# Spreading the closing averages and moments of a graph attention kernel over the last 47 steps of its softmax loop

## The chip, the cores and the metric

The kernel runs on one core of a Trainium2 chip. The metric is the device time of one execution in microseconds (us); shorter is better. PE is the matrix engine, DVE the vector engine, ACT the scalar engine, POOL is GpSimd and SP the engine that here only issues DMAs. PEld is the loading of weights into PE.

## What is computed

Two rounds of message passing over a graph with 6250 nodes and 100,000 edges, each followed by a layer normalisation over 128 features:

```python
edge_index = jnp.stack([src, dst])
x = _layernorm(x + _L0_gnn_ref(x, edge_attr_128, L0_gnn_fc_w, L0_gnn_attn, edge_type_100, src, dst), axis=-1)
x = _layernorm(x + _L1_gnn_ref(x, edge_index, L1_gnn_W, ...), axis=-1)
# the second round, in _L1_gnn_ref:
h = features @ W.T + b
s1 = h @ a1_w + a1_b[0]
s2 = h @ a2_w + a2_b[0]
e = s1[src] + s2[dst]
e = jnp.where(e >= 0, e, NEG_SLOPE * e)
m = jax.ops.segment_max(e, src, num_segments=n)
ex = jnp.exp(e - m[src])
denom = jax.ops.segment_sum(ex, src, num_segments=n)
att = ex / denom[src]
out = jax.ops.segment_sum(att[:, None] * h[dst], src, num_segments=n)
# and the normalisation:
m = jnp.mean(x, axis=axis, keepdims=True)
v = jnp.var(x, axis=axis, keepdims=True)
return (x - m) / jnp.sqrt(v + eps)
```

## The kernel before, in words

The first round (to about 1570 us of the profile) runs over 196 groups of 512 edges. Between the rounds the nodes are normalised in 52 blocks of 122 nodes each (`NS`, `BN`), multiplied with `W`, and written to `h_rows` in device memory; the normalised rows stay on chip in `xn`.

The second round, the softmax loop, starts at about 1614 us. The edges have been sorted by the block of their source node, and each block's edges are padded to whole groups of 512, so that a group belongs to one block, and the groups come in the order of the blocks. There are 208 groups here (832 gathers of 128 rows, four for each group). What each engine does in step g of this loop:

- POOL gathers the rows `h[dst]` of a group with four indirect DMAs (line 564, for the last 19 groups line 572). There are eight slots; the gather of group g waits until PE has finished step g - 5 (`step_done`).
- PE turns the scores of group g + 2 (line 910, `rows`), sends the maxima back to the edges (line 921, `back`), and sums the weighted rows of group g - 3 into PSUM (line 931, `attend`). `attend` of a group waits for ACT's weighted rows (`h_scaled`) and for DVE's update of the group before the last (`st_ready`).
- DVE begins with `update` of group g - 5 (line 1326): the block's running sum in `o_sb`, 128 features and the softmax denominator, is scaled by `decay` and the PSUM sum is added. The block's address is read into a register first (line 1321). Then come the running maximum (line 1359 and small instructions), the edge scores of group g - 2, the membership mask of group g + 2 (line 1316) and the one-hot rows of group g - 2 (`spread`, line 1401).
- ACT makes the penalties of group g + 2 (line 706), the exponentials of group g - 2 (`probs`, line 719), scales the gathered rows with them (`scale`, line 725, four instructions) and computes the decay of group g - 1 (line 713, also an exponential).
- SP loads the sorted sources of later groups (line 475).

When all groups of a block are summed, its result is closed in three steps: the average (the sum divided by the denominator, plus the old row in `xn`: a reciprocal and a scalar_tensor_tensor), the moments (`bn_stats`, `bn_aggr`), and the normalisation. For the normalisation ACT takes the square root of the variances of a run of blocks (line 769), DVE the reciprocal and the shift (`rates`, lines 1254 and 1255), and then both normalise blocks of the run: DVE those in `BY_DVE` (line 1502), ACT the others (line 772). In the first 32 blocks DVE has every fourth, behind them every second.

In the kernel before, DVE does averages and moments of blocks 0 to 31 inside its last 16 steps, two blocks a step (`early`, lines 1442, 1448, 1453), with two more calls of `early` behind the last step. Behind the loop and the last five updates come averages and moments of blocks 32 to 39, 40 to 47 and 48 to 51, each followed by the normalisation of the run before (`average` and `normalise`). ACT normalises nothing until its last decay is done.

The output is written in seven chunks of eight blocks (the last has four). A chunk's write waits until all its blocks are normalised by both engines (`fin_act`, `fin_dve`). SP writes 112 of the 122 rows of a block (line 503, 448 KB for a whole chunk), POOL the other ten (line 590), POOL behind its last gather.

All order is written out by hand: each engine's instructions run in the order of the code, and semaphores tie the engines together. The last steps of DVE, ACT and PE are unrolled behind a short loop whose length depends on the data.

## Time and profile before

| | us |
|---|---|
| median of 3 runs | 2707.32 (2706.15 to 2707.44) |
| the profiled execution | 2708.41, its span 2706.6 |
| busy in the span: PE, DVE, POOL, ACT | 2177.4, 2318.6, 1977.8, 1500.2 |
| softmax loop: first gather, last gather starts | 1614.4, 2652.3 |
| last update of a block's sum starts | 2675.08 |
| last normalisation starts | 2697.46 |

The profile is of one execution. Its engines' busy times are averages over two rounds with different limits, so the change has to be read in the last 250 us alone. The span leaves out some 1.8 us of the execution's own time.

### The profile page before, as it was taken

What the parts mean: (1) busy time and instruction counts of PE and PEld (TensorE: products, weight loads), DVE (VectorE), ACT (ScalarE), POOL (GpSimd) and SP (SyncE); (2) the same over time, 40 slices, a digit from 0 to 9 for tenths busy, and PEclk for the clock granted to TensorE, in tenths of its full rate; (3) what the DMA queues carried; (4) which work ended last, traced back from release to release, by engine and by line L of the source; (5) the groups of instructions that cost most, each with busy time, mean ns of one, the idle gap of its engine ahead of it and who ended that gap; (6) DMA issues with size and microseconds to landing.
All of it is one profiled execution on the core that took longest, in us unless ns stands there. A gap on an engine that the chain in (4) does not pass through costs nothing.

```text
span 2706.6 us, 42430 instructions
## 1 busy us (share of the span) xinstructions
PE 2177.4 (80%) x10869; PEld 1516.4 (56%) x10869; DVE 2318.6 (86%) x5886; ACT 1500.2 (55%) x3974; POOL 1977.8 (73%) x1839
## 2 busy tenths in 40 slices
PE   6999999999999999999999955666676666666663
PEld 3555555555555555555555545666565665666552
DVE  8999999999999999999999976666666666666786
ACT  2666666666666666666666644444444444444444
POOL 2477787777777777777777737777777777777772
PEclk8999999999999999999999976776767677767776
DMA  4233333333333333333333233333333333333332
GB/s 129 71 97 98 99 99 99 99 99 99 99 99 99 99 99 99 98 100 98 99 98 100 73 88 79 80 81 81 80 80 81 81 82 81 80 81 81 80 79 61
DMA packets 156587, 243.91 MB, mean 90 GB/s; under 512 B 40836, under 2 KB 84398, under 8 KB 156226
## 3 DMA queue, kind: packets, MB, share of 16 engines
q1 hardware_dynamic: 97730, 132.55, 17.5%
q0 software_dynamic: 58624, 108.72, 17.0%
q8 instruction: 89, 1.46, 0.2%
q14 instruction: 144, 1.18, 0.1%
HBM read 231.99 MB, written 9.12 MB: 89 GB/s over the span
## 4 chain that ended last, share of the span: by engine, by line
DVE 39%; issue 25%; POOL 18%; PE 7%; DMA 6%; DVEq 3%; ACT 1%; POOLq 0%; SPq 0%; ACTq 0%
POOL room L564 17%; DVE y L1169 16%; DVE hs L1177 9%; DMA room<-h_rows,y 5%; DVE room L1193 4%; PE FP L910 3%; DVEq L1149 2%; DVE room L1185 2%; POOL room L572 2%; PE AP L931 2%; DVE z L1162 1%; DVE accT L1153 1%; PE FP L931 1%; DVE doh L1134 1%; DVE joh L1143 1%
## 5 line engine op out<-in xcount | busy, mean ns | idle before, releaser
L520 POOL DMA_INDIRECT room<-in_x,pk x784 | 821.4, 1048 | 289.2 <-issue 279.4
L564 POOL DMA_INDIRECT room<-h_rows,y x756 | 713.5, 944 | 235.6 <-issue 217.3
L822 PE MATMUL FP<-fc_sb,room 128*128 128x512 f32 x1568 | 833.5, 613 | 2.2 <-issue 2.2
L831 PE MATMUL WP<-at_p,rel_oh 100*128 100x512 f32 x1568 | 804.9, 594 | 0.0
L628 ACT ACTIVATE w_sb<-WP 128x512 f32<-128x512 f32 x784 | 468.1, 597 | 516.2 <-PE WP L831 507.8
L910 PE MATMUL FP<-ident,room 128*128 128x128 f32 x1664 | 349.1, 375 | 366.9 <-DMA room<-h_rows,y 330.7
L910 PEld LDWEIGHTS FP<-ident,room 128*128 128x128 f32 x1664 | 296.0, 267 | 415.4 <-DMA room<-h_rows,y 368.0
L831 PEld LDWEIGHTS WP<-at_p,rel_oh 100*128 100x128 f32 x1568 | 298.3, 190 | 377.3 <-issue 377.3
L1162 DVE TENSOR_TENSOR z<-FP,w_sb 128x1024 f32<-128x1024 f32 x392 | 477.2, 1217 | 3.1 <-ACT w_sb L628 2.2
L706 ACT ACTIVATE accT<-accT,neg_big 128x512 f32<-128x512 bf16 x208 | 150.0, 722 | 559.5 <-DVE accT L1316 559.5
L1169 DVE SCALAR_TENSOR_TENSOR y<-z 128x2048 f32<-128x2048 f32 x196 | 446.4, 2278 | 0.0
L531 POOL DMA_INDIRECT sorted_edges<-runs,spot_i x196 | 352.7, 1800 | 93.5 <-issue 60.5
L822 PEld LDWEIGHTS FP<-fc_sb,room 128*128 128x128 f32 x1568 | 266.6, 190 | 43.4 <-issue 2.6
L841 PEld LDWEIGHTS AP<-doh,room 128*128 128x128 f32 x1568 | 191.3, 192 | 163.8 <-DVE room L1193 163.8
L841 PE MATMUL AP<-doh,room 128*128 128x64 f32 x1568 | 218.3, 282 | 79.7 <-DVE room L1193 76.2
L725 ACT ACTIVATE room<-room,pr 128x129 f32<-128x129 f32 x832 | 266.6, 392 | 6.8
L635 ACT ACTIVATE boh<-arena,rank_pay 128x52 f32<-128x52 bf16 x784 | 240.3, 379 | 0.0
L1177 DVE TENSOR_TENSOR hs<-y 128x1024 f32<-128x1024 f32 x196 | 238.2, 1215 | 0.0
L1326 DVE SCALAR_TENSOR_TENSOR arena<-arena,decay,AP 128x129 f32 x104 | 36.0, 347 | 185.5 <-PE AP L931 184.6
L1326 DVE SCALAR_TENSOR_TENSOR arena<-arena,decay,FP 128x129 f32 x104 | 36.0, 346 | 146.1 <-PE FP L931 143.3
L1359 DVE CUSTOM_DVE_ANT_0 hs<-accT,FP 128x512 f32<-128x512 f32 x208 | 141.7, 681 | 17.2 <-PE FP L910 12.0
L1316 DVE TENSOR_TENSOR accT<-z,WP 128x512 bf16<-128x512 bf16 x208 | 141.4, 680 | 0.8 <-DVE room L1309 0.8
(238 smaller groups left out, 2924.7 us busy)
## 6 DMA issues: line engine op xcount, KB each, us to landing
room<-in_e SPq DMA_DIRECT2D x196, 256.0 KB
rel_sb<-in_rel_g SPq DMA_DIRECT2D x196, 200.0 KB
z<-sorted_sources SPq DMA_DIRECT2D x208, 128.0 KB
room<-in_x,pk POOLq DMA_INDIRECT x784
room<-h_rows,y POOLq DMA_INDIRECT x756
sorted_edges<-runs,spot_i POOLq DMA_INDIRECT x196, 3.0
accT<-in_x_t SPq DMA_DIRECT2D x1, 3125.0 KB, 11.2
h_rows<-arena SPq DMA_DIRECT2D x13, 227.5 KB, 2.9
```

The lines of the kernel that those rows point to most:

```text
L520: pool.indirect_dma_start(xg[:, k, u, 0:P], None, x[:, :], bass.IndirectOffsetOnAxis(ap=pk[:, g, u:u + 1], axis=0)).then_inc(xg_in[k], 16)
L531: pool.indirect_dma_start(table[:, :], bass.IndirectOffsetOnAxis(ap=spot_i[:, g:g + 1], axis=0), runs[:, k, :], None).then_inc(sc_in[k], 16)
L564: pool.indirect_dma_start(hg[k][:, u, :], None, h_dram[:, :], bass.IndirectOffsetOnAxis(ap=sd[:, g * TG + u:g * TG + u + 1], axis=0)).then ...
L628: nc.scalar.activation(w_sb[:, u // 2, u % 2, :], WP[u % 2][:, :], ACT.Copy).then_inc(w_copied, 1)
L725: nc.scalar.activation(hg[k][:, u, 0:P + 1], hg[k][:, u, 0:P + 1], ACT.Identity, bias=0.0, scale=pr[:, k % 2, u:u + 1]).then_inc(h_scaled, 1)
L822: mm = pe.matmul(FP[u // 2][:, u % 2, :], e_sb[:, k, u, :], fc_sb[:, :], start=True, stop=True)
L831: mm = pe.matmul(WP[u % 2][:, :], rel_oh[:, k % 2, u * P:(u + 1) * P], at_p[:, j, :], start=(j == 0), stop=(j == 1))
L841: mm = pe.matmul(AP_[:, 0:W], msg[:, k % 2, u, :], doh[:, k % 2, u, :], start=(u == 0), stop=(u == TG - 1))
L910: mm = pe.matmul(rows_of(k)[:, u * P:(u + 1) * P], hg[k][:, u, P + 1:P + 2].to_broadcast([P, P]), ident[:, :], start=True, stop=True)
L1162: v.tensor_tensor(z[:, h, :, :], FP[h][:, :, :], w_sb[:, h, :, :], ALU.mult).then_inc(z_done, 1)
L1169: v.scalar_tensor_tensor(y[:, :, :, :], z[:, :, :, :], SLOPE0, z[:, :, :, :], ALU.mult, ALU.max).then_inc(y_done, 1)
L1177: v.tensor_tensor(hs[:, :, :], y_all[:, :, 0:D4 // 2], y_all[:, :, D4 // 2:D4], ALU.add).then_inc(hs_done, 1)
```

## The change

DVE's unrolled tail is 48 steps long now (`TAIL`), where it was 16; the unrolled steps ahead of its short loop are 32 fewer, so the count of steps is the same. In step j of the tail, from 1 to 47, `early(j - 1)` runs behind the step: it takes one block at each of four stages, its own small reciprocal of the denominator included (122x1, where it was one for the whole run of 32 blocks): the aggregation of block j - 4, the statistics of block j - 3, the average of block j - 2, and the weight of block j - 1. So blocks 0 to 43 are averaged and have their moments when the loop ends, and only blocks 44 to 51 remain.

The runs that share a square root are now 0 to 31, 32 to 43 and 44 to 51. The square root of the first run stands in ACT's step 200 (of 0 to 207), the first run's `rates` in DVE's step 202. ACT normalises four blocks in each of its steps 203 to 207, 20 of its 24, and DVE two in each of steps 203 to 206, all 8 of its own. The second run's square root comes behind ACT's last decay, and DVE's `rates` and six normalisations of that run stand between its update of group 205 and that of group 206. The last run is averaged and normalised behind the last update.

ACT's exponential and square root are in different tables, so ACT now loads a table three times where it did once (in this part of the program). What stands in ACT's row at step 200 and 201, after the change (line 715 is the decay, 708 the penalty, 721 `probs`, 760 the square root):

```order
L715 ACTIVATE decay<-dm 128x1 [waits st_ready]
L760 ACT_TABLE_LOAD
L760 ACTIVATE rstd<-mv,eps_col 122x32 [waits n_var]
L694 ISA [waits g_in6]
L694 ACTIVATE idx1<-y 128x4
L700 ISA [waits step_done]
L700 ACTIVATE mparts<-room 128x3
L705 REGISTER_ALU
L708 ACTIVATE accT<-accT,neg_big 128x512 [waits v_done,mT_ready]
L720 ISA [waits ed_ready]
L721 ACT_TABLE_LOAD
L721 ACTIVATE pr<-ed 128x4 [waits h_scaled]
```

The square root of the first run has moved here from behind the loop, with a load ahead of it and one ahead of the next exponential.

DVE's last step and the edges of the last two groups before (line 1442 averages, 1448 and 1453 moments, 1332 to 1352 the edges of group 206):

```order
L1401 TENSOR_TENSOR z<-WP0,y 128x512
L1442 SCALAR_TENSOR_TENSOR arena<-arena,rstd 122x128 x2
L1448 BN_STATS stats<-arena 122x6 [waits n_avg]
L1448 BN_STATS stats<-arena 122x6
L1453 BN_AGGR mv<-stats 122x2 [waits n_stat]
L1453 BN_AGGR mv<-stats 122x2
L1332 TENSOR_REDUCE sm<-EP 128x8 [waits step_done,ed_ready]
L1338 TENSOR_TENSOR el<-sm,room 128x4 [waits sm_read]
```

The same place after the change (line 1423 is `spread`, 1462 the aggregation):

```order
L1423 TENSOR_TENSOR z<-WP0,y 128x512
L1462 BN_AGGR mv<-stats 122x2 [waits n_stat]
L1354 TENSOR_REDUCE sm<-EP 128x8 [waits step_done,ed_ready]
L1360 TENSOR_TENSOR el<-sm,room 128x4 [waits sm_read]
```

Two averages, two statistics and one aggregation have left this place, and two statistics and four aggregations have left the place behind the edges.

DVE between the updates of groups 205 and 206 after the change (line 1348 is the update, 1276 and 1277 `rates`, 1480 the normalisation); before, the updates stood one behind the other:

```order
L1348 SCALAR_TENSOR_TENSOR arena<-arena,decay,FP1 128x129
L1276 RECIPROCAL rstd<-rstd 122x12 [waits n_std]
L1277 SCALAR_TENSOR_TENSOR nmr<-mv,rstd 122x12 [waits dve_step]
L1480 TENSOR_SCALAR arena<-arena,rstd,nmr 122x128 [waits n_rs]
L1480 TENSOR_SCALAR arena<-arena,rstd,nmr 122x128 x5
L1343 REGISTER_ALU
L1343 TENSOR_LOAD blk_i
L1343 ISA x2
L1344 REGISTER_ALU
L1348 ISA [waits st_ready,decay_ready,step_done]
L1348 SCALAR_TENSOR_TENSOR arena<-arena,decay,AP 128x129
```

The wait for ACT's square root (`n_std`) and eight instructions now stand ahead of the last two updates. ACT has four normalisations of the first run between its decay of group 206 and `probs` of group 206, where there was nothing.

```diff
--- before.py
+++ after.py
@@ -24,9 +24,10 @@
 NLAST = N - (NS - 1) * BN
 PMAIN = 112
 CHUNKS = [(q, min(q + 8, NS)) for q in range(0, NS, 8)]
-EARLY = 32
-RUNS = [(0, EARLY)] + [c for c in CHUNKS if c[0] >= EARLY]
-BY_DVE = [q for q in range(NS) if (q % 4 == 3 if q < EARLY else q % 2 == 1)]
+RUNS = [(0, 32), (32, 44), (44, NS)]
+EARLY = RUNS[1][1]
+TAIL = 48
+BY_DVE = [q for q in range(NS) if (q % 4 == 3 if q < RUNS[0][1] else q % 2 == 1)]
 BY_ACT = [q for q in range(NS) if q not in BY_DVE]
 HC = 4
 HCHUNKS = NS // HC
@@ -384,6 +385,7 @@
         step_done = sem("step_done")
         st_ready = sem("st_ready")
         n_avg = sem("n_avg")
+        n_weight = sem("n_weight")
         n_stat = sem("n_stat")
         s_out = sem("s_out")

@@ -752,25 +754,45 @@
                     idx(i + k + AHEAD, (k + AHEAD) % S1)
                     block_s1(i + k + AHEAD, (k + AHEAD) % S1, False)
                     step1(i + k, k, False)
+            def deviations(c):
+                q0, q1 = RUNS[c]
+                act.wait_ge(n_var, c + 1)
+                nc.scalar.activation(rstd[:, q0:q1], mv[:, q0:q1, 1], ACT.Sqrt,
+                                     bias=eps_col[0:BN, :]).then_inc(n_std, 1)
+
+            def normal(q):
+                nc.scalar.activation(xn[:, q, :], xn[:, q, :], ACT.Identity, bias=nmr[:, q:q + 1],
+                                     scale=rstd[:, q:q + 1]).then_inc(fin_act, 1)
+
+            mine = [[q for q in BY_ACT if q0 <= q < q1] for q0, q1 in RUNS]
             for k in range(S1):
                 if k < S1 - AHEAD:
                     idx(tail + (k + AHEAD), k + AHEAD)
                     block_s1(tail + (k + AHEAD), k + AHEAD, False)
                 step1(tail + k, k, False, k < S1 - 2)
+                if k == 0:
+                    deviations(0)
+                if k == 3:
+                    act.wait_ge(n_rs, 1)
+                if k >= 3:
+                    for q in mine[0][4 * (k - 3):4 * (k - 2)]:
+                        normal(q)
             for k in range(S1 - 2, S1):
                 probs(tail + k, k, False)
                 scale(tail + k, k, False)
             decays(tail + (S1 - 1), S1 - 1, False)


-            for c, (q0, q1) in enumerate(RUNS):
-                run = slice(q0, q1)
-                act.wait_ge(n_var, c + 1)
-                nc.scalar.activation(rstd[:, run], mv[:, run, 1], ACT.Sqrt, bias=eps_col[0:BN, :]).then_inc(n_std, 1)
-                act.wait_ge(n_rs, c + 1)
-                for q in [q for q in BY_ACT if q0 <= q < q1]:
-                    nc.scalar.activation(xn[:, q, :], xn[:, q, :], ACT.Identity, bias=nmr[:, q:q + 1],
-                                         scale=rstd[:, q:q + 1]).then_inc(fin_act, 1)
+            deviations(1)
+            for q in mine[0][4 * (S1 - 3):]:
+                normal(q)
+            act.wait_ge(n_rs, 2)
+            for q in mine[1]:
+                normal(q)
+            deviations(2)
+            act.wait_ge(n_rs, 3)
+            for q in mine[2]:
+                normal(q)


         @block.tensor
@@ -1432,46 +1454,58 @@
                 link(v.tensor_scalar(rstd[:, q0:q1], o_sb[:, q0:q1, P], 1.0e-30, None, ALU.max))
                 link(v.reciprocal(rstd[:, q0:q1], rstd[:, q0:q1]))

-            def early(j):
-
-                if j == 0:
-                    dve.wait_ge(st_ready, tail - LAG + 1)
-                    weights(0, EARLY)
-                if j < S1 * 2:
-                    for q in (2 * j, 2 * j + 1):
-                        ins = v.scalar_tensor_tensor(xn[:, q, :], o_sb[:, q, 0:P], rstd[:, q:q + 1], xn[:, q, :],
-                                                     ALU.mult, ALU.add)
-                    ins.then_inc(n_avg, 1)
-                if 1 <= j <= S1 * 2:
-                    dve.wait_ge(n_avg, j)
-                    for q in (2 * j - 2, 2 * j - 1):
-                        ins = v.bn_stats(stats[:, q, :], xn[:, q, :])
-                    ins.then_inc(n_stat, 1)
-                if j >= 2:
-                    dve.wait_ge(n_stat, j - 1)
-                    for q in (2 * j - 4, 2 * j - 3):
-                        ins = v.bn_aggr(mv[:, q, :], stats[:, q, :])
-                    if j == 2 * S1 + 1:
+            def early(i, g):
+
+                if 3 <= i:
+                    q = i - 3
+                    dve.wait_ge(n_stat, q + 1)
+                    ins = v.bn_aggr(mv[:, q, :], stats[:, q, :])
+                    if q + 1 in (RUNS[0][1], EARLY):
                         ins.then_inc(n_var, 1)
-
+                if 2 <= i < EARLY + 2:
+                    q = i - 2
+                    dve.wait_ge(n_avg, q + 1)
+                    v.bn_stats(stats[:, q, :], xn[:, q, :]).then_inc(n_stat, 1)
+                if 1 <= i < EARLY + 1:
+                    q = i - 1
+                    dve.wait_ge(n_weight, q + 1)
+                    v.scalar_tensor_tensor(xn[:, q, :], o_sb[:, q, 0:P], rstd[:, q:q + 1], xn[:, q, :], ALU.mult,
+                                           ALU.add).then_inc(n_avg, 1)
+                if i < EARLY:
+                    dve.wait_ge(st_ready, g - LAG + 1)
+                    link(v.tensor_scalar(rstd[:, i:i + 1], o_sb[:, i, P:P + 1], 1.0e-30, None, ALU.max))
+                    v.reciprocal(rstd[:, i:i + 1], rstd[:, i:i + 1]).then_inc(n_weight, 1)
+
+            def normal(q):
+                v.tensor_scalar(xn[:, q, :], xn[:, q, :], rstd[:, q:q + 1], nmr[:, q:q + 1], ALU.mult,
+                                ALU.add).then_inc(fin_dve, 1)
+
+            mine = [[q for q in BY_DVE if q0 <= q < q1] for q0, q1 in RUNS]
             more = group_count(dve)
-            tail = dve.snap(more + (G1_LEAST - 2 * S1))
+            tail = dve.snap(more + (G1_LEAST - TAIL))
             members(0, 0, True)
             members(1, 1, True)
             for k in range(S1):
                 step1(k, k, True, k, k - 2)
-            for g in range(S1, G1_LEAST - 3 * S1):
+            for g in range(S1, G1_LEAST - TAIL - S1):
                 step1(g, g % S1, False, g % S1, (g - 2) % S1)
-            with dve.Fori(G1_LEAST - 3 * S1, dve.snap(more + (G1_LEAST - 3 * S1 + D1 + 1)), D1) as i:
+            with dve.Fori(G1_LEAST - TAIL - S1, dve.snap(more + (G1_LEAST - TAIL - S1 + D1 + 1)), D1) as i:
                 half = dve.snap(i & (S1 - D1))
                 other = dve.snap(S1 - 2 - half)
                 for k in range(D1):
                     step1(i + k, k, False, half + k, half + (k - 2) if k >= 2 else other + k)
-            for j in range(2 * S1):
+            for j in range(TAIL):
                 k = j % S1
-                step1(tail + j, k, False, k, (k - 2) % S1, j < 2 * S1 - 2)
-                early(j)
-            for j in range(2 * S1 - 2, 2 * S1):
+                step1(tail + j, k, False, k, (k - 2) % S1, j < TAIL - 2)
+                if j >= 1:
+                    early(j - 1, tail + j)
+                if j == TAIL - 6:
+                    rates(1, slice(*RUNS[0]))
+                    dve.wait_ge(n_rs, 1)
+                if j >= TAIL - 5:
+                    for q in mine[0][2 * (j - TAIL + 5):2 * (j - TAIL + 6)]:
+                        normal(q)
+            for j in range(TAIL - 2, TAIL):
                 last = (tail + j, j % S1, False)
                 dve.wait_ge(ed_ready, tail + j)
                 edge_parts(*last)
@@ -1479,9 +1513,13 @@
                 edge_lrelu(*last)
                 edge_shift(*last)
                 spread(*last)
-            early(2 * S1)
-            early(2 * S1 + 1)
-            for j in range(2 * S1 - LAG, 2 * S1):
+            for j in range(TAIL - LAG, TAIL - 2):
+                update(tail + j, j % S1, False)
+            rates(2, slice(*RUNS[1]))
+            dve.wait_ge(n_rs, 2)
+            for q in mine[1]:
+                normal(q)
+            for j in range(TAIL - 2, TAIL):
                 update(tail + j, j % S1, False)


@@ -1494,19 +1532,12 @@
                 link(ins)
                 moments(q0, q1)

-            def normalise(c):
-                q0, q1 = RUNS[c]
-                rates(c + 1, slice(q0, q1))
-                dve.wait_ge(n_rs, c + 1)
-                for q in [q for q in BY_DVE if q0 <= q < q1]:
-                    v.tensor_scalar(xn[:, q, :], xn[:, q, :], rstd[:, q:q + 1], nmr[:, q:q + 1], ALU.mult,
-                                    ALU.add).then_inc(fin_dve, 1)
-
             dve.wait_ge(st_ready, dve.snap(more + G1_LEAST))
-            for c in range(1, len(RUNS)):
-                average(*RUNS[c])
-                normalise(c - 1)
-            normalise(len(RUNS) - 1)
+            average(*RUNS[2])
+            rates(3, slice(*RUNS[2]))
+            dve.wait_ge(n_rs, 3)
+            for q in mine[2]:
+                normal(q)


 def kernel(x, src, dst, edge_attr_128, edge_type_100, L0_gnn_fc_w, L0_gnn_attn, L1_gnn_W, L1_gnn_b, L1_gnn_a1_w,
```

## Rows read from the trace of the kernel before

**Rows 1.** The page: shares of the chain that ended last, by line

```profile
POOL room L564 17%; DVE y L1169 16%; DVE hs L1177 9%; DMA room<-h_rows,y 5%; DVE room L1193 4%; PE FP L910 3%; DVEq L1149 2%; DVE room L1185 2%; POOL room L572 2%; PE AP L931 2%; DVE z L1162 1%; DVE accT L1153 1%; PE FP L931 1%; DVE doh L1134 1%; DVE joh L1143 1%
```

**Rows 2.** Gathers, by line: count, duration ns min/median/max, first and last start us

```profile
L572 POOL DMA_INDIRECT room<-h_rows,idx x76: 940/944/1067, 2558.4 to 2652.3; - x76
...
L564 POOL DMA_INDIRECT room<-h_rows,y x756: 940/944/1047, 1614.4 to 2557.2; - x189
```

**Rows 3.** Stretches: us, busy PE PEld DVE ACT POOL (instructions), clock, DMA, GB/s

```profile
2460.00:2558.00 98.00, 64.69 (x400) 59.43 (x399) 68.17 (x339) 43.78 (x155) 74.22 (x79) 0.72 0.39 80
2558.00:2654.00 96.00, 60.67 (x380) 55.70 (x380) 80.46 (x405) 46.90 (x172) 72.15 (x77) 0.73 0.38 75
```

**Rows 4.** DVE timeline, steps 201 to 203: start us, us, instruction

```profile
2633.34 0.61 DVE L1442 SCALAR_TENSOR_TENSOR arena<-arena,rstd 122x128 f32<-122x128 f32 x2
...
2634.26 0.23 DVE L1453 BATCH_NORM_AGGREGATE mv<-stats 122x2 f32<-122x6 f32 x2
2634.41 0.32 DVE L1326 SCALAR_TENSOR_TENSOR arena<-arena,decay,FP 128x129 f32 x1
...
2638.80 0.32 DVE L1326 SCALAR_TENSOR_TENSOR arena<-arena,decay,AP 128x129 f32 x1
```

**Rows 5.** DVE timeline behind the loop: weights of four blocks, their average

```profile
2691.98 0.16 DVE L1432 TENSOR_SCALAR rstd<-arena 122x4 f32<-122x4 f32 x1
2692.18 0.18 DVE L1433 RECIPROCAL rstd<-rstd 122x4 f32<-122x4 f32 x1
2692.39 1.14 DVE L1492 SCALAR_TENSOR_TENSOR arena<-arena,rstd 122x128 f32<-122x128 f32 x4
```

**Rows 6.** The chain in order of time: the last gather, start to landing

```profile
2652.29 4.78 DMA room<-h_rows,idx
```

**Rows 7.** ACT timeline, last step and behind it

```profile
2664.80 0.19 ACT L713 ACTIVATE decay<-dm 128x1 f32<-128x1 f32 x1
...
2667.44 1.28 ACT L725 ACTIVATE room<-room,pr 128x129 f32<-128x129 f32 x4
2669.55 0.20 ACT L713 ACTIVATE decay<-dm 128x1 f32<-128x1 f32 x1 [0.82 <-DVE arena L1326]
2669.77 1.28 ACT L769 ACT_TABLE_LOAD   x1
2671.06 0.32 ACT L769 ACTIVATE rstd<-mv,eps_col 122x32 f32<-122x32 f32 x1
...
2680.95 9.34 ACT L772 ACTIVATE arena<-arena,nmr,rstd 122x128 f32<-122x128 f32 x24 [9.57 <-DVE nmr L1255]
...
2696.73 0.28 ACT L769 ACTIVATE rstd<-mv,eps_col 122x4 f32<-122x4 f32 x1
2697.46 0.88 ACT L772 ACTIVATE arena<-arena,nmr,rstd 122x128 f32<-122x128 f32 x2 [0.44 <-DVE nmr L1255]
```

**Rows 8.** DVE timeline, from behind `spread` of step 207 to the first closing run

```profile
2663.95 0.60 DVE L1442 SCALAR_TENSOR_TENSOR arena<-arena,rstd 122x128 f32<-122x128 f32 x2
...
2665.02 0.15 DVE L1332 TENSOR_REDUCE sm<-EP 128x8 f32<-128x24 f32 x1
...
2667.65 0.48 DVE L1448 BATCH_NORM_STATS2 stats<-arena 122x6 f32<-122x128 f32 x2
...
2669.10 0.35 DVE L1326 SCALAR_TENSOR_TENSOR arena<-arena,decay,FP 128x129 f32 x1 [0.69 <-issue]
...
2671.80 0.35 DVE L1326 SCALAR_TENSOR_TENSOR arena<-arena,decay,FP 128x129 f32 x1 [1.39 <-PE FP L931]
...
2675.08 0.35 DVE L1326 SCALAR_TENSOR_TENSOR arena<-arena,decay,FP 128x129 f32 x1 [1.21 <-PE FP L931]
...
2679.81 0.64 DVE L1248 BATCH_NORM_AGGREGATE mv<-stats 122x2 f32<-122x6 f32 x8
```

**Rows 9.** Output tensor: POOL's writes, from issue to landing

```profile
DMA to landing us min/median/max: 3.5/3.6/3.9
```

**Rows 10.** A stretch of output writes, columns as in Rows 3

```profile
2684.00:2688.00 4.00, 0.00 (x0) 0.00 (x0) 3.93 (x23) 4.00 (x12) 0.90 (x2) 0.50 0.81 208
```

## The prediction

> **What bounds the kernel now.** I read the chain of waits first. By line, POOL's gathers of the softmax loop have the largest share, and the gathers' DMAs a further part [rows 1]. The gathers themselves say why: 832 of them start between 1614.4 and 2652.3 us, one every 1.249 us, and each takes 0.944 [rows 2]. Four make a group, so a step of the loop lasts 5.00 us, whatever the others do as long as they keep up. Next the stretches. In 98 us ahead of the last 19 groups (19.6 steps) DVE is busy 68.17 us and ACT 43.78, that is 3.5 and 2.2 us a step, and in the 96 us behind them DVE 80.46 us, 4.2 a step, ACT 46.90, and POOL's pace is unchanged [rows 3]. So DVE has a free microsecond and more in each step, and what is put there costs nothing while the gathers set the pace. What costs in full stands behind the last landing, at about 2657.1 [rows 6]: from there to 2698.34 only DVE, ACT and a few sums of PE work, and most of it is averages, moments and normalisations [rows 7, 8]. In the DVE timeline the reader is to see that between the last update (2675.08) and the last normalisation (2697.46) the loop is over, and that only closing work is left.
>
> **The work put into the loop.** Now DVE has one block a step in 44 of the last 47 steps, where it had two in the last 16. Two blocks cost 1.07 us (2633.34 to 2634.41), and a step with them that waits for nothing 4.39 (2634.41 to 2638.80), so a step without them 3.32 [rows 4]. One average and one statistics are half of 0.92 (2633.34 to 2634.26), 0.46; an aggregation is 0.08. New are a small clamp and a reciprocal for each block, which stand 0.20 and 0.21 us from the next instruction [rows 5]. That makes 0.95 a block, and a step of 4.27 us. Steps 203 to 206 have two normalisations besides, at the average's 0.28 each [rows 5], 4.84; step 202 has `rates`, two small instructions at 0.2, 4.7. All are below 5.00. In steps 161 to 191 the cover is DVE's wait for PE; steps 192 to 207 become lighter than they were, apart from the four.
>
> ACT has 2.4 to 2.8 us free in a step [rows 3]. In step 200 it takes a table load and a root, 1.6 us, in step 201 the load back, 1.28 ahead of the exponential [rows 7]; from step 203 on four normalisations at 9.34/24 = 0.389, 1.56 us. PE needs the scaled rows only in the next step, so all of this fits. I cost it at 0. If the cover were gone the two loads would delay one step by up to 1.3 us.
>
> The Trainium skill ("ScalarE: Activation LUTs", section "What ACT_TABLE_LOAD costs") adds a drain of about 1.38 us to each switch of sets. In the row the load starts at 2669.77 and the root at 2671.06, 1.29 later [rows 7], with nothing between them, so the trace doesn't show such a drain here and the sum goes without it. With it the root of the second run would be 1.4 us later, and by the order of DVE's instructions the last two updates as well; the gain would be 13.6 us instead of 15.0.
>
> **From the last landing to the last update.** I keep the times of before as a clock. Behind `spread` of step 207 DVE has one aggregation, 0.08, where two blocks took 2663.95 to 2665.02. The edges of groups 206 and 207 take 2.63 us (to 2667.65), so they end at 2666.7. Two statistics and four aggregations are gone behind them too. Before, the update of group 203 stood 0.69 us behind the instruction ahead of it, in reading its address; so it comes at about 2667.4, where it came at 2669.10 [rows 8]. It had held PE's sums, so these move up by 1.7. The update of 205 followed 2.70 us behind that of 203, and comes at 2670.1; that of 207 followed 5.98 behind, and could come at 2673.4.
>
> But now something stands ahead of it. ACT ends its decay of group 206 at about 2664.9, as before, then has four normalisations to 2666.5, two times an exponential and four scalings (0.2 + 1.28) to 2669.4, the last decay (0.22 to the next), the load 1.29 and the root 0.3: the second run's root is there at 2671.2 [rows 7]. The scaled rows of 207 at 2669.4 are in time for PE's last sum, which starts after 2671. DVE waits for the root from 2670.5 on, then `rates` 0.4 and six normalisations 1.7, to 2673.3; the update of 206 comes 0.7 later and that of 207 a further 1.0, at 2675.0 against 2675.08. The 1.7 us won are spent on work that stood behind the loop. Bounds: 2673.6, if the address reads hide as they do inside a step, and 2676.4, with 1.4 us for a later root.
>
> **Behind the last update.** Before, 2675.08 to 2698.34 (2697.46 + 0.88), 23.26 us. Now the update, averages and moments of eight blocks, which are what stood there first: to 2680.45, 5.37 us [rows 8]. ACT is free then; from its root to the first normalisation 0.73, and four of them 1.65 [rows 7], with 0.05 for the signal. Sum 7.80. The gain is 23.26 - 7.80 = 15.46, with the 0.08 above 15.5.
>
> **The output.** POOL's last write lands 3.6 us after its issue [rows 9], and the end of the span follows as before. Twelve blocks are now written at the end, where it was four and a chunk 1.5 us ahead of them. A chunk of 448 KB takes 448/208 = 2.2 us of the DMA engines [rows 10]; it can go two ACT normalisations, 0.8 us, before the end, and the small chunk takes 0.8 more, so they are through about when POOL's write lands. I take 0, between -0.2 and +1.5. At the other end there is a new meeting. Chunk 0 can be written from ACT's step 204 on, at about 2650, while the last gathers are under way, and the last took 4.78 us to land [rows 6]. All that stands behind it moves with it. At worst the whole chunk goes ahead, 2.2 us; at best nothing happens. I take 0.5, as the DMA engines are busy 0.38 in that stretch [rows 3].
>
> Sum: 15.5 - 0.5 = 15.0 us. The profiled execution (2708.41, span 2706.6) would be 2693.4, its span 2691.6; from the median 2707.32, which is 1.1 below it, 2692.3.
>
> **Rivals.** (a) The end gives back more: the first writes cost the last gather 2.2 us, the last writes 1.5, the root comes late by 1.4. For it speaks that all three are new meetings, against it that each is bounded by a row: 15.5 - 5.1, about 2697.
>
> (b) The slower side: the loop doesn't hide the blocks. DVE's idle time is not spread evenly; it waits for PE, and PE for DVE's maxima. If 0.95 us went into each of the 32 steps from 160 to 191, they would be 30 us longer, and the kernel 15 slower, 2722. It decides from where DVE's step and its wait exceed 5.00 us, and half of the effect would already undo the gain. Against it: with 1.07 us more in each of 16 steps the gathers kept 0.944 and their pace to the end [rows 2, 3].
>
> (c) DVE slows POOL itself. The 12 more averages and the eight normalisations in the loop each hold up a gather for their own length, 0.28 us and at most 0.35: 20 such are 6 to 7 us, 2699. The rows of before show gathers of 0.944 with averages beside them (line 572) and without (line 564) [rows 2], so I give it little. The Trainium skill ("SBUF — State Buffer", section "Who interferes with whom") has such a rule: a DVE instruction with two SBUF inputs, as the average is, contends with a GpSimd instruction that reads SBUF, and the second one waits; by that rule (c) is what happens, and the rows 2 don't show it.
>
> (d) The change gives almost nothing, as the DMA of the output sets the end: 6250 rows of 512 bytes are 3.2 MB, at 208 GB/s [rows 10] 15.4 us, and before they began when ACT had done six of its 24, at 2683.3 [rows 7]. If the first chunks were held until then, the time would be 2706 or so. Against it: three or four chunks can be written before the last update now, and they need 2.2 us each.
>
> **Chances.** The forecast 0.75, (a) 0.13, (b) 0.03, (c) 0.06, (d) 0.03. The forecast's own range is 2690 to 2695.5; with (a) and half of (c), and with 1.5 us below for address reads and sums of PE that hide better, 2689 to 2698.5. About 5.4 us, 0.2%, can be told from no change here. Faster 0.95, same 0.02, slower 0.03.
>
> **What would show it.** Right: gathers still 1.249 us apart up to a last one near 2652.3; DVE's steps 161 to 191 with about 1 us less idle time; the last update at 2675 give or take 1.5; three closing groups of instructions where there were four; the last normalisation ending about 15.5 us earlier. A last landing later than 2658 is the write of chunk 0. A gather pace above 1.25 in 2410 to 2560 would make the prediction wrong at its base, and show (b) if POOL then waits for PE, (c) if the gathers themselves are longer.

## The result and the profile after

| | before | after |
|---|---|---|
| median of 6 runs, us | 2706.78 (2705.88 to 2707.44) | 2691.80 (2690.23 to 2692.39) |
| ratio of the times | | 0.9943, 95% interval 0.9931 to 0.9956 |
| profiled execution, us (span) | 2708.41 (2706.6) | 2690.23 (2688.4) |
| first gather to last gather of the loop | 1037.9 | 1038.6 |
| last gather to PE's first use of it | 4.90 | 4.94 |
| from there to the start of the last update | 17.89 | 16.72 |
| to the end of the last normalisation | 23.26 | 7.84 |
| to the end of the span | 8.26 | 8.43 |

The medians are 15.0 us apart, as predicted. The two profiled executions are 18.2 apart: that of after is among its fastest runs, and its loop began 2.5 us earlier, in a part that the change doesn't touch. What the change touches, the last five lines of the table, sums to 15.7.

The gathers, their counts and durations (ns, shortest, median, longest), then first and last start, against [rows 2]:

```profile
L566 POOL DMA_INDIRECT room<-h_rows,y x756: 940/944/1069, 1611.9 to 2555.0; - x189
...
L574 POOL DMA_INDIRECT room<-h_rows,idx x76: 940/944/1069, 2556.3 to 2650.5; - x76
```

They last 0.944 us as before. The stretches of [rows 3], same columns:

```profile
2460.00:2558.00 98.00, 59.91 (x381) 55.13 (x380) 80.75 (x425) 43.80 (x156) 74.23 (x79) 0.75 0.38 80
2558.00:2654.00 96.00, 65.18 (x380) 59.85 (x380) 80.34 (x424) 50.75 (x176) 71.57 (x76) 0.68 0.39 75
```

DVE is busy 80.75 us where it was 68.17, and POOL's share has not moved. So the work is hidden. But the DVE timeline of one step of the tail shows how narrowly; where [rows 4] had the update right behind the aggregation, now this stands there:

```profile
2563.40 0.17 DVE L1462 BATCH_NORM_AGGREGATE mv<-stats 122x2 f32<-122x6 f32 x1
2563.49 0.26 DVE L1468 BATCH_NORM_STATS2 stats<-arena 122x6 f32<-122x128 f32 x1
2563.67 0.34 DVE L1472 SCALAR_TENSOR_TENSOR arena<-arena,rstd 122x128 f32<-122x128 f32 x1
2563.92 0.15 DVE L1476 TENSOR_SCALAR rstd<-arena 122x1 f32<-122x1 f32 x1
2564.10 0.16 DVE L1477 RECIPROCAL rstd<-rstd 122x1 f32<-122x1 f32 x1
2565.04 0.35 DVE L1348 SCALAR_TENSOR_TENSOR arena<-arena,decay,FP 128x129 f32 x1 [0.78 <-issue]
...
2570.07 0.35 DVE L1348 SCALAR_TENSOR_TENSOR arena<-arena,decay,AP 128x129 f32 x1 [0.78 <-issue]
```

The reader is to look at the last column: 0.78 us of idle time that no engine ends. From update to update it is 5.03 us, where 4.27 was predicted and the gathers' pace is 5.00. Whom DVE waited for, from 2460 to 2556 us (total, times, longest), says the same; before, these were PE, 17.7 and 11.9 us:

```profile
DVE arena L1348 <- issue: 13.2, 17, 0.8
DVE arena L1348 <- ACT decay L715: 1.1, 1, 1.1
DVE arena L1348 <- PE FP L953: 0.8, 1, 0.8
```

The end on ACT, against [rows 7] (line 764 normalises, 760 is the load and the root):

```profile
2663.35 1.63 ACT L764 ACTIVATE arena<-arena,nmr,rstd 122x128 f32<-122x128 f32 x4
...
2667.91 1.28 ACT L760 ACT_TABLE_LOAD   x1
2669.20 0.30 ACT L760 ACTIVATE rstd<-mv,eps_col 122x12 f32<-122x12 f32 x1
...
2678.32 1.65 ACT L764 ACTIVATE arena<-arena,nmr,rstd 122x128 f32<-122x128 f32 x4 [0.47 <-DVE nmr L1277]
```

And on DVE, against [rows 8]: the updates of groups 203 to 207, with `rates` and six normalisations ahead of the last two, then the end of the only averaged run that is left:

```profile
2665.47 0.35 DVE L1348 SCALAR_TENSOR_TENSOR arena<-arena,decay,FP 128x129 f32 x1 [0.26 <-issue]
2667.27 0.35 DVE L1348 SCALAR_TENSOR_TENSOR arena<-arena,decay,AP 128x129 f32 x1 [1.45 <-issue]
2668.27 0.35 DVE L1348 SCALAR_TENSOR_TENSOR arena<-arena,decay,FP 128x129 f32 x1 [0.65 <-ACT decay L715]
2669.54 0.23 DVE L1276 RECIPROCAL rstd<-rstd 122x12 f32<-122x12 f32 x1 [0.92 <-ACT rstd L760]
...
2670.01 1.63 DVE L1480 TENSOR_SCALAR arena<-arena,rstd,nmr 122x128 f32<-122x128 f32 x6
2671.55 0.34 DVE L1348 SCALAR_TENSOR_TENSOR arena<-arena,decay,AP 128x129 f32 x1
2672.13 0.35 DVE L1348 SCALAR_TENSOR_TENSOR arena<-arena,decay,FP 128x129 f32 x1 [0.24 <-DVE arena L1348]
...
2676.87 0.64 DVE L1270 BATCH_NORM_AGGREGATE mv<-stats 122x2 f32<-122x6 f32 x8
```

The 23 us of closing work have become one run of eight blocks, 7.84 us.

### The profile page after: what moved, and what is told of

Read it like the earlier page. It is cut to its first block, busy times and chain, and to the rows that moved or that the text cites. A ratio compares the mean times of both kernels' runs of the same rounds, so it can differ in the third digit from the quotient of the medians.

```text
span 2688.4 us, 42671 instructions
## 1 busy us (share of the span) xinstructions
PE 2172.6 (81%) x10869; PEld 1513.3 (56%) x10869; DVE 2332.1 (87%) x5966; ACT 1501.8 (56%) x3975; POOL 1977.9 (74%) x1839
## 4 chain that ended last, share of the span: by engine, by line
DVE 42%; issue 26%; POOL 18%; PE 5%; DMA 4%; DVEq 4%; ACT 0%; POOLq 0%; SPq 0%; ACTq 0%
POOL room L566 18%; DVE y L1191 16%; DVE hs L1199 9%; DVE room L1215 4%; DMA room<-h_rows,y 4%; DVEq L1171 2%; PE FP L932 2%; DVE room L1207 2%; DVE accT L1175 2%; DVE z L1184 1%; PE FP L953 1%; DVE doh L1156 1%; PE AP L953 1%; DVE joh L1165 1%; DVE arena L1026 1%
## 5 line engine op out<-in xcount | busy, mean ns | idle before, releaser
L1381 DVE CUSTOM_DVE_ANT_0 hs<-accT,FP 128x512 f32<-128x512 f32 x208 | 142.1, 683 | 17.7 <-PE FP L932 11.7
L617 ACT ACTIVATE rel_abs<-rel_sb,neg_col 100x512 f32<-100x512 int32 x196 | 139.7, 713 | 0.1
```

## The experiments

Each was compared with the kernel before on its own chip: the first four on one chip, the four from full_c on a second, the four from skew on a third. "Tail" is the time from the start of the last gather to the end of the last normalisation in the profile: 46.05 us before, 29.5 after.

| run | median | before there | difference | ratio, 95% interval |
|---|---|---|---|---|
| full_b | 2924.02 | 2934.06 | -10.0 | 0.9947 to 0.9975 |
| avg32_b | 2930.46 | 2934.06 | -3.6 | 0.9976 to 0.9994 |
| norm_behind_b | 2927.84 | 2934.06 | -6.2 | 0.9969 to 0.9987 |
| mid_behind_b | 2926.20 | 2934.06 | -7.9 | 0.9959 to 0.9980 |
| full_c | 2691.84 | 2707.68 | -15.8 | 0.9927 to 0.9954 |
| act_late | 2691.89 | 2707.68 | -15.8 | 0.9929 to 0.9956 |
| early48 | 2686.43 | 2707.68 | -21.2 | 0.9911 to 0.9938 |
| more3 | 2726.58 | 2707.68 | +18.9 | 1.0054 to 1.0085 |
| skew | 2691.12 | 2706.00 | -14.9 | 0.9930 to 0.9957 |
| skew_more3 | 2692.02 | 2706.00 | -14.0 | 0.9932 to 0.9962 |
| skew48 | 2688.15 | 2706.00 | -17.8 | 0.9917 to 0.9944 |
| hold_writes | 2692.32 | 2706.00 | -13.7 | 0.9935 to 0.9963 |

**The first four, on a slower chip.** The changed kernel itself, and three that each undo one part of it.

> The changed kernel itself, as the base for the three others on the same chip. Expected 2691.8, within 1 us.

> The changed kernel, but blocks 32 to 43 get their averages and moments behind the last update again, all else in the loop as it is now. My theory, that closing work behind the loop counts in full and in the loop nothing: 12 blocks at 0.275 + 0.207 + 0.08 us are 6.7, the weights 0.4, and six normalisations of DVE move behind the last update too, less about 1 us because nothing stands ahead of the last two updates: 7 to 8 us more, about 2699.5. The rival, that the gain comes from normalising in the loop and not from the averages: at most 2 us more, 2694.

```diff
-EARLY = RUNS[1][1]
+EARLY = RUNS[0][1]
...
-            rates(2, slice(*RUNS[1]))
-            dve.wait_ge(n_rs, 2)
-            for q in mine[1]:
-                normal(q)
...
+            average(*RUNS[1])
             average(*RUNS[2])
+            rates(2, slice(*RUNS[1]))
+            dve.wait_ge(n_rs, 2)
+            for q in mine[1]:
+                normal(q)
```

> The changed kernel, but nothing is normalised in the loop, and the root of the first run stands behind the last decay: ACT has 24 and 6 blocks to normalise, 30 x 0.389 = 11.7 us, ahead of its last root, DVE 8 more ahead of the last two updates. My theory: ACT sets the end, 4 to 6 us more, about 2697. The rival (averages carry all of the gain, ACT had time enough anyway): no more than 1 us, 2692.5.

```diff
-                if k == 0:
-                    deviations(0)
-                if k == 3:
-                    act.wait_ge(n_rs, 1)
-                if k >= 3:
-                    for q in mine[0][4 * (k - 3):4 * (k - 2)]:
-                        normal(q)
...
+            deviations(0)
             deviations(1)
-            for q in mine[0][4 * (S1 - 3):]:
+            act.wait_ge(n_rs, 1)
+            for q in mine[0]:
                 normal(q)
```

(and on DVE `rates` and eight normalisations of the first run behind the update of group 205)

> The changed kernel, but DVE's rates and six normalisations of the second run stand behind its last update instead of ahead of the last two. My theory: the last update comes 1.1 us earlier, the moved 2.0 us come behind it, so 0.9 us more, about 2692.7. The rival (the wait for the root ahead of the updates costs more than it hides): 0.5 to 1 us less, 2691.

```diff
-            rates(2, slice(*RUNS[1]))
-            dve.wait_ge(n_rs, 2)
-            for q in mine[1]:
-                normal(q)
             for j in range(TAIL - 2, TAIL):
                 update(tail + j, j % S1, False)
+            rates(2, slice(*RUNS[1]))
+            dve.wait_ge(n_rs, 2)
+            for q in mine[1]:
+                normal(q)
```

This chip is 227 us slower with every kernel, and the base was not what I expected. In the same 100 us of the loop, first of the profile after, then of full_b (columns as [rows 3]):

```profile
1900.00:2000.00 100.00, 65.79 (x415) 60.69 (x414) 65.54 (x343) 45.76 (x160) 75.62 (x81) 0.75 0.35 81
```

```profile
1900.00:2000.00 100.00, 61.99 (x336) 54.92 (x335) 55.60 (x289) 38.98 (x137) 63.06 (x68) 0.64 0.32 68
```

A step takes about 6 us. TensorE has 0.64 of its clock where it had 0.75, so it is at its lower level (1.2 GHz) more often. POOL waits, where on the other chip it only had its 0.30 us between gathers. In full_b, by what ended the idle time ahead of the gathers (us, times):

```profile
  issue: 218.7, 671
  remote: 141.3, 57
  PE AP L953: 45.5, 14
  PE FP L953: 24.5, 14
```

So there the gathers don't set the pace alone, and the change brings 10.0 us. I have no profile of the kernel before on that chip, so where the other 5 us are is not shown. Between kernels of this chip: putting 12 blocks' averages back behind the loop costs 6.4 us in the medians and 8.5 in the tail (33.8 to 42.3), as the first theory said. Putting the normalisations back costs 3.8 in the medians, just below the 4 to 6 that were expected, but only 1.4 in the tail, so where the rest of it lies is not shown; and the intervals of full_b and norm_behind_b overlap a little, so the size is uncertain. Moving `rates` and six normalisations behind costs 2.2 and 0.5; the sign agrees with the 0.9 expected, the size is inside the scatter.

**On chips that run the kernels in the times of the result: base, ACT's chain, more blocks, more load.**

> The changed kernel again, as the base for the three others on their chip. If the chip grants TensorE about 0.87 of its clock over the span, as in the two profiles of the prediction, 2692 and 15 us less than before; if it grants 0.81, as in the last four runs, 2924 and 10 us less.

It was 2691.84, 15.8 below before.

> The changed kernel, but ACT's four normalisations of its last step stand behind its last decay and the root of the second run. In the profile of the changed kernel DVE waits 0.92 us for that root ahead of the last two updates. My theory, that this ACT chain is what holds the last update: the root comes 1.5 us earlier, the last update 0.9, the end 0.9. The rival, that PE's last sums hold it: no difference (under 0.3 us).

```diff
-                if k >= 3:
+                if 3 <= k < S1 - 1:
                     for q in mine[0][4 * (k - 3):4 * (k - 2)]:
...
-            for q in mine[0][4 * (S1 - 3):]:
+            for q in mine[0][4 * (S1 - 4):]:
```

No gain in the time. But the root did come earlier, and DVE no longer waits for it. The last three updates (here the last gather started at 2652.07):

```profile
2669.89 0.35 DVE L1348 SCALAR_TENSOR_TENSOR arena<-arena,decay,FP 128x129 f32 x1 [1.40 <-PE FP L953]
2672.16 0.34 DVE L1348 SCALAR_TENSOR_TENSOR arena<-arena,decay,AP 128x129 f32 x1
2673.46 0.35 DVE L1348 SCALAR_TENSOR_TENSOR arena<-arena,decay,FP 128x129 f32 x1 [0.96 <-DVE arena L1348]
```

The update of 206 starts 20.1 us behind the last gather, where it was 21.1 in the profile after: 1.0 us earlier, where the theory gave 0.9. So ACT's chain did hold it; now what ends a wait there is PE's sum, ahead of the update of 205. But 0.96 us stand ahead of the last update, where it was 0.24: one read of an address took 1.14 us there. It began at 2671.72, 1.3 us behind the start of an output write (2670.37). So the last update started 21.4 us behind the last gather, against 21.7, and of the 1.0 us only 0.3 came.

> Blocks 0 to 47 are averaged in the loop (a tail of 56 steps, the runs 0 to 31, 32 to 47, 48 to 51), and ACT's four last normalisations moved as in act_late. My theory: four blocks less behind the last update are 2.3 us of averages and moments and 0.8 of ACT's normalisations, two more normalisations of DVE ahead of the last updates cost 0.5, and 0.9 for act_late: 3.5 us less than the changed kernel. The rival, that four more blocks in the loop are not hidden or the last writes of the output take the place: no gain over the changed kernel.

```diff
-RUNS = [(0, 32), (32, 44), (44, NS)]
+RUNS = [(0, 32), (32, 48), (48, NS)]
-TAIL = 48
+TAIL = 56
...
-                if j >= 1:
-                    early(j - 1, tail + j)
+                if j >= 5:
+                    early(j - 5, tail + j)
```

(with the edit of act_late). The closing run on ACT and DVE:

```profile
2676.26 0.35 DVE L1348 SCALAR_TENSOR_TENSOR arena<-arena,decay,FP 128x129 f32 x1 [0.46 <-PE FP L953]
...
2679.15 0.38 DVE L1270 BATCH_NORM_AGGREGATE mv<-stats 122x2 f32<-122x6 f32 x4
```

```profile
2680.30 0.88 ACT L764 ACTIVATE arena<-arena,nmr,rstd 122x128 f32<-122x128 f32 x2 [0.45 <-DVE nmr L1277]
```

From the last update to the end it takes 4.9 us, where it was 7.84, and the tail is 26.8, where full_c has 29.4: 2.6 us less, of 3.5 expected. An address read of 1.16 us stands ahead of the last update here too. The median is 5.4 less than that of full_c, but the runs fall in two clusters (2686.0 to 2686.4, and 2689.1, 2690.8), and the medians of such few runs move with them. The two profiles, the slowest run of each kernel, have loops of nearly the same length (1040.2 and 1040.1), so the 2.6 of the tail is the better measure.

> The changed kernel with three more averages of a block in each of 44 steps of the loop, into a tile that nothing reads (0.26 us each, two inputs in SBUF like the real ones). A DVE step that waits for nothing becomes 4.2 + 0.8 = 5.0 us. If DVE's work in the loop is free up to the gathers' pace of 5.00 us (my theory): 0 to 3 us more. If each average in the loop holds up a gather (rival c): 132 x 0.26 = up to 34 us more and gathers longer than 0.944. If DVE's work adds to PE's waits long before that (rival b): 10 to 30 us more with POOL waiting for PE.

```diff
+                    for k in range(3):
+                        v.scalar_tensor_tensor(fc_sb[0:BN, k * P:(k + 1) * P], o_sb[:, q, 0:P], rstd[:, q:q + 1], cen[0:BN, :], ALU.mult,
+                                               ALU.add)
```

It took 34.7 us more than full_c, where my theory gave 0 to 3: all of the added time is on the path. It is neither rival as I had put them. The gathers keep their length, so it is not (c):

```profile
L566 POOL DMA_INDIRECT room<-h_rows,y x756: 938/944/1092, 1614.5 to 2567.1; - x189
```

And DVE's steps:

```profile
2603.37 0.16 DVE L1480 RECIPROCAL rstd<-rstd 122x1 f32<-122x1 f32 x1
2604.29 0.35 DVE L1348 SCALAR_TENSOR_TENSOR arena<-arena,decay,AP 128x129 f32 x1 [0.76 <-ACT decay L715]
...
2610.03 0.35 DVE L1348 SCALAR_TENSOR_TENSOR arena<-arena,decay,FP 128x129 f32 x1 [0.76 <-ACT decay L715]
```

A step of DVE is 5.74 us, which is 4.98 of instructions and the 0.76 ahead of the update; 44 steps at 0.74 above the pace are 33 us. The delay reaches POOL as rival (b) has it: from 2450 to 2650 us PE waits 65.3 us for DVE's maximum (L1381) and POOL 20.4 us for PE's sums. But it sets in with a step of DVE above 5.00 us, not long before. The trace puts this idle time down to ACT's decay, as the last of the update's waits, but that decay belongs to a group four steps back; the same 0.76 is "issue" elsewhere. So the question became where the 0.78 us comes from.

**The pair of clamp and reciprocal.** The reciprocal waits, by a semaphore, for the clamp just ahead of it. The address of the next update is read by the same queue, and in the trace that read starts only when the queue has got past the wait; in [rows 4] no instruction waited for the one just ahead of it, and the read was over before the averages. The read of the step shown above, behind the reciprocal that started at 2564.10 (line 1343 is the read; count, ns, first and last start):

```profile
L1343 DVEq TENSOR_LOAD <-blk_i x1: 307/307/307, 2564.2 to 2564.2; - x1
```

It takes 0.31 us, and what the queue has to do behind it is done at 2565.04, when the update starts.

> The changed kernel, but the reciprocal of a block's weight stands a step behind its clamp, so that no instruction of DVE waits for the one just ahead of it. In the profile of the changed kernel DVE's address read starts only behind that wait, and the update comes 0.78 us behind it in each step: a step of DVE lasts 5.03 us where it waits for nothing else. New theory: this pair holds up DVE's queue; a step becomes about 4.25 us, DVE waits for PE again, and the loop gets 0.7 us shorter, as its gathers were held 1038.6 us against 1037.9 before; the median 0.5 to 1 us less, 2691. The rival (the 0.78 us are a price of the longer unrolled tail or of the more registers, not of the pair): the step stays at 5.03.

```diff
+                if 1 <= i < EARLY + 1:
+                    q = i - 1
+                    dve.wait_ge(n_clamp, q + 1)
+                    v.reciprocal(rstd[:, q:q + 1], rstd[:, q:q + 1]).then_inc(n_weight, 1)
                 if i < EARLY:
                     dve.wait_ge(st_ready, g - LAG + 1)
-                    link(v.tensor_scalar(rstd[:, i:i + 1], o_sb[:, i, P:P + 1], 1.0e-30, None, ALU.max))
-                    v.reciprocal(rstd[:, i:i + 1], rstd[:, i:i + 1]).then_inc(n_weight, 1)
+                    v.tensor_scalar(rstd[:, i:i + 1], o_sb[:, i, P:P + 1], 1.0e-30, None, ALU.max).then_inc(n_clamp, 1)
```

(the average, statistics and aggregation a step further back each, `early(j, tail + j)` in every step). In a step of it the next update follows with no idle time, and the read of its address (the last line) stands 1.3 us ahead of the reciprocal:

```profile
2547.63 0.15 DVE L1478 RECIPROCAL rstd<-rstd 122x1 f32<-122x1 f32 x1
...
2547.75 0.34 DVE L1349 SCALAR_TENSOR_TENSOR arena<-arena,decay,AP 128x129 f32 x1
```

```profile
L1344 DVEq TENSOR_LOAD <-blk_i x1: 316/316/316, 2546.3 to 2546.3; - x1
```

Whom DVE waited for from 2460 to 2556 us:

```profile
DVE arena L1349 <- PE AP L954: 9.9, 6, 2.3
DVE arena L1349 <- PE FP L954: 8.2, 6, 3.4
```

The "issue" is gone, and DVE waits for PE again. First to last gather takes 1037.9 us, as before; in the five profiles with the pair and no added work (after, full_c, act_late, early48, hold_writes) it took 1038.0 to 1040.2, and in skew48, again without the pair, 1038.1. Most of that scatter (817.8 to 819.7 us) lies ahead of the last 44 steps, where the kernels do the same work. The last 176 gathers alone, 44 steps, take 220.0 us before, 220.2 to 220.7 in the five with the pair (220.7 after), and 220.0 and 220.1 in skew and skew48. So the pair costs up to 0.7 us of the loop, and without it that is gone. The median, 14.9 below before, can't be told from that of the changed kernel.

> Three more averages in each of 44 steps as before, with the reciprocal a step behind. By the new theory DVE's step falls from 5.8 to 4.25 + 0.78 = 5.03 us, the gathers' pace, and of the 35 us that the three averages cost, all but 0 to 3 are gone: about 2693. If the stall is not the pair's: 2726 again. If averages themselves hold up gathers or PE: 10 us or more stay.

```profile
2539.87 0.33 DVE L1349 SCALAR_TENSOR_TENSOR arena<-arena,decay,AP 128x129 f32 x1
...
2543.66 0.87 DVE L1476 SCALAR_TENSOR_TENSOR fc_sb<-arena,rstd,cen 122x128 f32<-122x128 f32 x3
2544.45 0.16 DVE L1481 RECIPROCAL rstd<-rstd 122x1 f32<-122x1 f32 x1
2544.53 0.13 DVE L1484 TENSOR_SCALAR rstd<-arena 122x1 f32<-122x1 f32 x1
2544.75 0.35 DVE L1349 SCALAR_TENSOR_TENSOR arena<-arena,decay,FP 128x129 f32 x1
```

A step with the three averages is 4.88 us, below the pace, and the kernel 2692.02: 0.9 us more than skew on the same chip. Of the 34.7 us all but one are gone, by moving one tiny instruction. This settles it: averages in this loop are all but free while DVE's step is shorter than 5.00 us, and the pair alone had used up the margin.

> The candidate for the best version: 48 blocks averaged in the loop, ACT's four last normalisations behind the root, and the reciprocal a step behind. Expected 5.4 us less than the changed kernel, as measured of the first two, and 0.5 to 1 more for the third: about 2686. The rival, that the third gives nothing: as it was without it, 2686.4.

It was 2688.15, 17.8 below before, with a tail of 26.0. Expected was 2686. This and early48 are the best versions, and their intervals overlap, so the third edit can't be seen in the time.

**The writes of the output.**

> The changed kernel, but SP and POOL write no chunk of the output before ACT has normalised all its 24 blocks of the first run, at about 2671. In the profile of the changed kernel the update of group 204 came 1.8 us behind that of 203 where it had been 0.96, beside the write of chunk 2, and DVE's address read took 1.15 us once where it takes 0.30. Theory: the write slows the read, so here it is 0.30 again and the last update 0 to 0.8 us earlier; behind it five chunks of 2.0 us each from 2671.5 on end at about 2682 and the last two at 2685, 1.5 to 2 us later than now: 1 to 1.5 us more in all. The rival (d), that the end is set by the writes: 5 us more or worse.

```diff
+            sp.wait_ge(fin_act, 24)
             for q0, q1 in CHUNKS:
                 full = min(q1, NS - 1)
...
```

(the same on POOL). The updates of groups 203 and 204:

```profile
2665.36 0.35 DVE L1350 SCALAR_TENSOR_TENSOR arena<-arena,decay,FP 128x129 f32 x1 [0.26 <-issue]
2666.31 0.35 DVE L1350 SCALAR_TENSOR_TENSOR arena<-arena,decay,AP 128x129 f32 x1 [0.60 <-DVE arena L1350]
```

They are 0.95 us apart again, where it was 1.80. But the last update came 22.0 us behind the last gather, not earlier (21.7): the root was still at its place, and DVE waited for it instead. The writes ran without a gap from 2671.1 to about 2686, and the span ended 9.7 us behind the last normalisation, where it was 8.4. The median is 2692.32, within the scatter of the changed kernel's. So rival (d) isn't so: even held back by 18 us, the writes cost 1.3 us at the end.

## Why the prediction was right, by its steps

The mechanism was right: what moved under the loop left the path, and what stayed behind the last update took its predicted time. That the total came out to the tenth is in part luck, as the errors of the steps went both ways.

- *The work put into the loop costs nothing.* Right to 0.7 us (1038.6 against 1037.9), but by luck to that extent: there was next to no margin. The step of 4.27 us was wrong: the clamp and the reciprocal were priced at 0.20 and 0.21 us from two rows behind the loop [rows 5], where no address read follows. The wait between them made the next step's read late, 0.78 us, and the step 5.03, 0.03 above the pace. The prediction asked what is queued behind an added wait for the root at the end, not for this pair in the loop. skew and skew_more3 show it. The sign that was named for a wrong base, a gather pace above 1.25 us from 2410 to 2560, is just met: 1.252 after, 1.249 before. It is too small to cost more than the 0.7 us.
- *Rival (b).* Its point of decision, a step of DVE above 5.00 us, is what more3 shows; not through PE's waits but through DVE's own queue. With the pair the changed kernel stood at that point.
- *Rival (c).* Gathers kept 0.944 us with 132 more averages of two SBUF inputs. By the Trainium skill's rule ("SBUF — State Buffer", section "Who interferes with whom"), as the prediction applied it to the gathers, the second of the two would wait. Neither more3 nor skew_more3 shows a longer gather, nor a longer average: three last 0.87 us there, four 1.14 behind the loop [rows 5].
- *From the last landing to the last update.* Predicted 17.8 us, measured 16.72. The root was done 14.1 us behind PE's first use, predicted 14.0; there was no drain ahead of it, 1.29 us from load to root as before. `rates` and the six normalisations took 2.0, predicted 2.1. What was mis-sized are the address reads behind them: the update of 206 was put 0.7 us behind the normalisations and that of 207 a further 1.0, and measured are 0 and 0.58, as the reads hid behind the six normalisations. That is 0.3 above the lower bound that was named. (On the profile's own clock the last update came at 2672.13, outside the 2675 give or take 1.5, since the loop began 2.5 us earlier.)
- *Behind the last update.* Predicted 7.80, measured 7.84. Gain 15.42 of the predicted 15.46.
- *The meetings with the writes.* At the front 0.5 was taken and 0.04 came (4.94 against 4.90): ACT's step 204, measured from the last gather, ran some 4 us later than before (2649.6 where it was 2647.1, with the last gather 1.8 earlier), so the first write began at 2652.7, when the last gather had been issued 2.3 us before. At the end 0 was taken and 0.17 came. The table loads cost nothing in the loop.

In sum, against the forecast gain: -0.7 in the loop, +0.5 and +1.1 up to the last update, -0.2 at the end. With the prediction's 15.0 that is 15.7 in the profile; the medians say 15.0.

## What to carry to other kernels

Closing work that is moved under a loop costs next to nothing up to the point where its engine's step reaches the loop's pace, and here it cost in full beyond it; so price the whole step, with its waits, and compare it with the pace. An instruction that waits for the one just ahead of it can be dear not for itself but for what its queue can't start early: here one reciprocal of 122 numbers cost as much as three averages. Put such pairs a step apart. A profile of a kernel that gained what was expected can still show a margin of nothing; look for idle time that no engine ends.

## What the runs showed besides

One chip ran all kernels in 2924 to 2934 us (medians) where on the others they took 2686 to 2708 (2727 with the added load), with a lower granted clock and waits of POOL that the trace calls "remote" (141.3 us in full_b); what sends them is open.

DVE's read of an address from SBUF takes 0.30 us as a rule. It took 1.08 to 1.33 us at the longest in each of the eight profiles of the other chips in which output was written beside the last reads (after, full_c, act_late, early48, more3, skew, skew_more3, skew48). In the two in which nothing was, before and hold_writes, it took at most 0.32 in the whole loop. In these eight each read of more than 1 us began 0.9 to 1.5 us behind the start of one of SP's output writes. On the slower chip the longest beside a write are 0.62 to 1.06 us, but there reads of 0.47 to 0.70 stand near 2510 to 2610 us too, where no output is written. So a write as the cause fits all profiles, as the only cause it does not; how it acts is not shown.
